# Second attention of a four-layer block: 64x64 products in quarters of the array, probabilities scaled instead of outputs, and a new order on every engine

## The reference

```python
qh = (q @ Wq).reshape(b, l, HEADS, HEAD_DIM).transpose(0, 2, 1, 3)
kh = (kv @ Wk).reshape(b, s, HEADS, HEAD_DIM).transpose(0, 2, 1, 3)
vh = (kv @ Wv).reshape(b, s, HEADS, HEAD_DIM).transpose(0, 2, 1, 3)
qh = rms_norm(qh, q_norm_w)
kh = rms_norm(kh, k_norm_w)
scores = jnp.einsum('bhld,bhsd->bhls', qh, kh) * (1.0 / np.sqrt(HEAD_DIM))
scores = jnp.where(mask, scores, NEG_INF)
attn = jax.nn.softmax(scores, axis=-1)
o = jnp.einsum('bhls,bhsd->bhld', attn, vh)
o = o.transpose(0, 2, 1, 3).reshape(b, l, HEADS * HEAD_DIM)
return o @ Wo
```

## Time and profile before

| | |
|---|---|
| median of 3 runs | 2405.72 us (2403.03 to 2406.18) |
| the profiled execution | 2402.11 us, span 2400.1 us |
| TensorE busy | 2088.1 us, 87% of the span |
| VectorE / ScalarE / GpSimd busy | 69% / 37% / 26% |
| the second attention | about 845 to 1380 us of the span |

### The profile page before, as it was taken

How to read it: one execution, slowest core, us unless ns; L and a number is a source line. 1 busy time by engine, 2 the same in 40 slices (tenths; PEclk the granted TensorE clock), 3 DMA queues, 4 the chain that set the end, 5 groups by cost and what they waited for, 6 DMA issues and landing times. The chain is left out here.

```text
span 2400.1 us, 39365 instructions
## 1 busy us (share of the span) xinstructions
PE 2088.1 (87%) x12809; PEld 1146.2 (48%) x12811; DVE 1658.4 (69%) x3378; ACT 881.2 (37%) x1559; POOL 613.7 (26%) x832
## 2 busy tenths in 40 slices
PE   4759999999999879999999899689979999768965
PEld 2634444444444446666666544245544444324531
DVE  4857776786787767777777589567746666436668
ACT  4522212201211056666666554223332222223335
POOL 4641110111111054545555332222200000111201
PEclk8569999999999989999999999789979999979985
DMA  3403203221320421111111000000003433210001
GB/s 103 149 1 72 55 19 70 54 62 26 71 54 17 107 85 35 33 34 32 35 31 36 23 1 1 1 12 12 11 19 94 109 80 84 56 27 13 12 3 36
DMA packets 131760, 106.43 MB, mean 44 GB/s; under 512 B 95400, under 2 KB 113704, under 8 KB 127152
## 3 DMA queue, kind: packets, MB, share of 16 engines
q1 hardware_dynamic: 131632, 104.84, 17.8%
HBM read 80.85 MB, written 2.97 MB: 35 GB/s over the span
## 5 line engine op out<-in xcount | busy, mean ns | idle before, releaser
L1020 PE MATMUL l0f_acc<-l0f_z,w_all 128*128 128x512 f32 x512 | 232.0, 615 | 22.7 <-DVE l0f_z L1232 22.7
L917 POOL TENSOR_TENSOR l0f_v<-l0f_val,l0f_top 64x256 f32<-64x256 f32 x128 | 78.4, 613 | 505.3 <-DVE l0f_val L1195 497.8
L971 PE MATMUL l0f_work<-w_all,l0f_xs 128*128 128x512 f32 x384 | 183.5, 600 | 9.9 <-DVE l0f_val L1190 8.6
L1020 PEld LDWEIGHTS l0f_acc<-l0f_z,w_all 128*128 128x128 f32 x512 | 100.2, 197 | 153.8 <-issue 126.0
L241 POOL TENSOR_SCALAR var_eps<-mean_var 128x4 f32<-128x4 f32 (+1 forms) x64 | 14.6, 229 | 540.6 <-DVE mean_var L225 538.8
L2268 PE MATMUL a_score<-keys_by_head,a_qT 128*64 128x512 f32 x512 | 143.0, 640 | 9.0 <-DMA keys_by_head<-w_all 9.0
L1195 DVE COPY_PREDICATED l0f_val<-l0f_oh,l0f_work 128x512 f32<-128x512 int32 x160 | 116.7, 729 | 23.7 <-PE l0f_work L971 7.5
L2760 DVE TENSOR_TENSOR l2f_hu<-l2f_act_g,l2f_pu 128x512 f32<-128x512 f32 x104 | 71.2, 685 | 68.8 <-ACT l2f_act_g L2686 67.5
L2686 ACT ACTIVATE l2f_act_g<-l2f_pg 128x512 f32<-128x512 f32 x104 | 61.5, 594 | 149.6 <-PE l2f_pu L2627 137.7
L2635 PE MATMUL l2f_acc<-l2f_hid,w_all 128*128 128x512 f32 x208 | 107.4, 598 | 10.4 <-DVE l2f_hid L2766 10.4
L1690 DVE TENSOR_REDUCE l1x_ms_k<-l1x_sq_k 128x8 f32<-128x512 f32 x64 | 43.9, 687 | 103.2 <-ACT l1x_sq_k L1576 103.2
(11 more groups left out here) (360 smaller groups left out, 4811.3 us busy)
## 6 DMA issues: line engine op xcount, KB each, us to landing
l0f_first_mask<-onehots SPq DMA_DIRECT2D x32, 512.0 KB, 5.7
w_all<-onehots SPq DMA_DIRECT2D x32, 512.0 KB, 11.8
l1x_v<-l1x_vr SPq DMA_DIRECT2D x256, 64.0 KB, 2.1
w_all<-combination SPq DMA_DIRECT2D x40, 256.0 KB, 5.2
w_all<-in_weights SPq DMA_DIRECT2D x1, 4640.0 KB, 17.4
l0x_m_b<-running_max SPq DMA_DIRECT2D x16, 256.0 KB, 4.6
keys_by_head<-w_all SPq DMA_DIRECT2D x256, 8.0 KB
keys_by_head<-ctxT_all SPq DMA_DIRECT2D x256, 8.0 KB
```

The costliest lines, as they stand in the source:

```text
L917: nc.gpsimd.tensor_tensor(v2[a * SEQ:(a + 1) * SEQ, t % 2, b, :, :], val[r, t % 2, :, :].rearrange("p (c a) k -> p c a k", a=2)[:, :, a, : ...
L971: nc.tensor.matmul(value_banks[e % 3][:, :], xs[:, t * P:(t + 1) * P], ve[:, e, :], start=True, stop=True).then_inc(ve_done, 1)
L1020: nc.tensor.matmul(acc[:, :], oe[:, n % E, n // E, :], z[:, n % Z, :], start=(n == 0), stop=(n == C * E - 1)).then_inc(acc_done, 1)
```

## The change

Scores: kT is a plain copy, and each head's 64x64 block is a product of its own, 64 input rows and 64 output partitions, 16 in all; the two heads of a chunk go to two banks of `score`. The mask is two instructions, one a bank. Values: the output comes out turned, straight from 16 products of 64x64x64 of `v2` and the turned probabilities, so `turn_out` and `og` go; therefore the probabilities are scaled (`scale_probs`) and not the outputs. The outputs share a PSUM bank with the projected v (`v_and_out`), so `project_v` of n waits for `copy_oT` of n-4, and `values` of n-3 for `copy_v` of n. The probabilities are turned into k's bank `turn1` and no longer into q's. `prob` has two buffers, `vr` and `v2` four. The zeroed tiles and their memsets go. The order on TensorE, ScalarE and VectorE is new; GpSimd's is the same.

```diff
--- before.py
+++ after.py
@@ -1288,23 +1288,22 @@
...
-        qT, kb = sb("qT", [P, C, P]), sb("kb", [P, C, 2, 2, SEQ])
-        vr = sb("vr", [P, 2, W])
-        v2 = sb("v2", [P, 2, 2, C, 2, HD])
+        qT, kT = sb("qT", [P, C, P]), sb("kT", [P, C, P])
+        vr = sb("vr", [P, 4, W])
+        v2 = sb("v2", [P, 4, 2, C, HD])
-        diff, prob = sb("diff", [P, HU, SEQ]), sb("prob", [P, HU, SEQ])
+        diff, prob = sb("diff", [P, HU, SEQ]), sb("prob", [P, 2, HU, SEQ])
-        og = sb("og", [P, HU, HD])
-        proj_q, proj_k, proj_v = ps("proj_q"), ps("proj_k"), ps("proj_v")
-        turn0, turn1, score, po, y = ps("turn0"), ps("turn1"), ps("score"), ps("po"), ps("y")
+        proj_q, proj_k, v_and_out = ps("proj_q"), ps("proj_k"), ps("v_and_out")
+        turn0, turn1, y = ps("turn0"), ps("turn1"), ps("y")
...
@@ -1334,17 +1333,16 @@
...
-                sp.wait_ge(v2_zero, count(2))
-                    after(sp, pv_done, n - 1)
+                    after(sp, pv_done, n - 3)
-                            sp.dma_start(v2[a * SEQ:(a + 1) * SEQ, j % 2, b, :, a, :],
-                                         vr[b * SEQ:(b + 1) * SEQ, j % 2, :].rearrange("p (c a e) -> p c a e", c=C, a=2)
-                                         [:, :, a, :]).then_inc(v_loaded[j % 2], 16)
+                            sp.dma_start(v2[a * SEQ:(a + 1) * SEQ, j % 4, b, :, :],
+                                         vr[b * SEQ:(b + 1) * SEQ, j % 4, :].rearrange("p (c a e) -> p c a e", c=C, a=2)
+                                         [:, :, a, :]).then_inc(v_loaded[j % 4], 16)
...
@@ -1416,7 +1412,8 @@
...
                     after(pe, vr_ready, n)
-                    nc.tensor.matmul(proj_v[:, :], cs[:, j // 4, tok], wv[:, h * W:(h + 1) * W], start=True, stop=True)\
+                    after(pe, oT_ready, n - 3)
+                    nc.tensor.matmul(v_and_out[:, :], cs[:, j // 4, tok], wv[:, h * W:(h + 1) * W], start=True, stop=True)\
...
-                    after(pe, pT_ready, n - 1)
-                    after(pe, oT_ready, n - 2)
+                    pe.wait_ge(pT_ready, count(max(n - 1, 0) if isinstance(n, int) else n - 1))
...
@@ -1450,49 +1446,44 @@
-                    nc.tensor.matmul(score[:, :], core.ident_bf[:, :],
-                                     bcast(mask[:, bass.ds(4 * g + j // 2, 1), :].rearrange("p one k -> p (one k)"), 1, HU),
-                                     start=True, stop=False, skip_group_check=True)
+                    key_mask = mask[:, bass.ds(4 * g + j // 2, 1), :].rearrange("p one k -> p (one k)")
+                    for a in range(2):
+                        nc.tensor.matmul(score[:, a, :], core.ident_bf[:, :], bcast(key_mask, 1, C),
+                                         start=True, stop=False, skip_group_check=True)
                     for c in range(C):
                         for b in range(2):
-                            q = slice(b * SEQ, (b + 1) * SEQ)
-                            ins = nc.tensor.matmul(score[q, c * P:(c + 1) * P], qT[:, c, q],
-                                                   kb[:, c, b, :, :].rearrange("p a k -> p (a k)"),
-                                                   start=False, stop=True, skip_group_check=True)
+                            for a in range(2):
+                                r, q = slice(a * HD, (a + 1) * HD), slice(b * SEQ, (b + 1) * SEQ)
+                                ins = nc.tensor.matmul(score[q, a, c * SEQ:(c + 1) * SEQ], qT[r, c, q], kT[r, c, q],
+                                                       start=False, stop=True, skip_group_check=True)
                     ins.then_inc(score_done, 1)
 
-                def turn_probs(n):
-                    pe.wait_ge(exp_done, count(n + 1))
-                    pe.wait_ge(qT_ready, count(at_most(n + 2, U * GROUPS)))
+                def turn_probs(g, j):
+                    n = U * g + j
+                    pe.wait_ge(prob_ready, count(n + 1))
+                    pe.wait_ge(kT_ready, count(at_most(n + 2, U * GROUPS)))
                     after(pe, pT_ready, n)
                     for c in range(C):
-                        ins = nc.tensor.transpose(turn0[:, c * P:(c + 1) * P],
-                                                  prob[:, 2 * c:2 * c + 2, :].rearrange("p a k -> p (a k)"),
+                        ins = nc.tensor.transpose(turn1[:, c * P:(c + 1) * P],
+                                                  prob[:, j % 2, 2 * c:2 * c + 2, :].rearrange("p a k -> p (a k)"),
                                                   core.const("ident"))
                     ins.then_inc(p_turned, 1)
 
                 def values(g, j):
                     n = U * g + j
                     pe.wait_ge(pT_ready, count(n + 1))
-                    pe.wait_ge(v_loaded[j % 2], 64 * (4 * g + j // 2 + 1))
-                    after(pe, og_ready, n)
+                    pe.wait_ge(v_loaded[j % 4], 64 * (2 * g + j // 4 + 1))
+                    pe.wait_ge(vr_ready, count(at_most(n + 4, U * GROUPS)))
+                    after(pe, oT_ready, n)
+                    pe.sem_inc(may_multiply, 1)
                     for c in range(C):
                         for b in range(2):
-                            q = slice(b * SEQ, (b + 1) * SEQ)
-                            ins = nc.tensor.matmul(po[q, c * P:(c + 1) * P], probT[:, c, q],
-                                                   v2[:, j % 2, b, c, :, :].rearrange("p a e -> p (a e)"),
-                                                   start=True, stop=True)
+                            for a in range(2):
+                                r = slice(a * SEQ, (a + 1) * SEQ)
+                                q = slice(b * SEQ, (b + 1) * SEQ)
+                                ins = nc.tensor.matmul(v_and_out[r, c * P + b * SEQ:c * P + (b + 1) * SEQ], v2[r, j % 4, b, c, :],
...
-                def turn_out(n):
...
                 def slot(g, j):
                     if live(g):
                         project_q(g, j)
+                    h, i = lagging(g, j, 3)
+                    if live(h):
+                        turn_probs(h, i)
+                    if live(g):
+                        project_v(g, j)
                     h, i = lagging(g, j, 1)
                     if live(h):
                         turn_q(U * h + i)
+                        turn_k(U * h + i)
+                    h, i = lagging(g, j, 3)
+                    if live(h):
+                        values(h, i)
                     if j % 4 in (3, 0):
                         h, i = lagging(g, j, 7)
                         if live(h):
                             project_out(h, i)
-                    if live(g):
-                        project_v(g, j)
-                    h, i = lagging(g, j, 1)
-                    if live(h):
-                        turn_k(U * h + i)
                     if j % 4 == 1:
...
-                    h, i = lagging(g, j, 2)
-                    if live(h):
-                        turn_probs(U * h + i)
-                    h, i = lagging(g, j, 3)
-                    if live(h):
-                        turn_out(U * h + i)
                     h, i = lagging(g, j, 1)
                     if live(h):
                         scores(h, i)
-                    h, i = lagging(g, j, 2)
-                    if live(h):
-                        values(h, i)
 
                 for g in range(2):
                     for j in range(U):
...
@@ -1584,69 +1570,62 @@
                 def copy_kT(n):
                     act.wait_ge(k_turned, count(n + 1))
                     after(act, score_done, n)
-                    for a in range(2):
-                        r = slice(a * HD, (a + 1) * HD)
-                        ins = nc.scalar.activation(kb[r, :, :, a, :],
-                                                   turn1[r, :].rearrange("p (c b k) -> p c b k", c=C, b=2), ACT.Copy,
-                                                   scale=core.col("l1_kw")[r, :])
-                    ins.then_inc(kT_ready, 1)
+                    nc.scalar.activation(kT[:, :, :], turn1[:, :].rearrange("p (c k) -> p c k", c=C), ACT.Copy,
+                                         scale=core.col("l1_kw")).then_inc(kT_ready, 1)
 
...
                 def copy_v(g, j):
                     n = U * g + j
                     act.wait_ge(v_done, count(n + 1))
-                    if not isinstance(g, int) or n > 1:
-                        act.wait_ge(v_loaded[j % 2], 64 * (4 * g + j // 2))
-                    nc.scalar.activation(vr[:, j % 2, :], proj_v[:, :], ACT.Copy).then_inc(vr_ready, 1)
-
-                def exp(n):
+                    if not isinstance(g, int) or n > 3:
+                        act.wait_ge(v_loaded[j % 4], 64 * (2 * g + j // 4))
+                    nc.scalar.activation(vr[:, j % 4, :], v_and_out[:, :], ACT.Copy).then_inc(vr_ready, 1)
+
+                def exp(g, j):
+                    n = U * g + j
```

(60 more changed lines are left out.)

33 lines of the change are left out of this document (13 added, 20 removed).

## The result

The changed kernel takes 2455.64 us (median of 4, 2452.2 to 2457.96) beside 2404.38 us for the kernel before (median of 4 on the same chip): ratio 1.0212, 95% interval 1.0194 to 1.023, so 1.9 to 2.3% slower. The profiled execution's span is 2455.2 us, 55.1 above that of before.

A forecast was written before the change was run, and what follows sets the result against it. VectorE's new order was taken to put both root trips in series: mean slot 8.54 us against 7.88, +42 us, plus 4.5 for half clock, giving 2448.6, or 2452 us as a median. The range was 2425 to 2490 us.

The forecast's parts named there:

- The slot: Second attention, eight heads of a 128-token tile: mean slot 8.54 us against 7.88, +42 us over 64 slots.
- The loop without projection: VectorE's order with q's and k's root trips through GpSimd in series, in slots without output projection: 8.47 us.
- The slots with a projection: Path from normalise k through turned keys, values, output projection and k's square to k's root: 8.61 us a slot.
- Values: TensorE's 16 products of 64x64x64 for the values: 1.08 us from start to next, +.10.
- Scores: TensorE's scores in four quadrants instead of two column halves: between .46 and 1.08 us, no effect on the time.
- TensorE's own queue: TensorE's work without waits: 6.9 to 7.5 us a slot; at 7.2, a 43 us gain if it still bounded.
- the faster rival: TensorE stays the bound from `project_q` to `scores` and the kernel is faster: -43 us, 2363 us; chance .09.
- busy share: TensorE waits before the turned keys for normalise k and is busy some 83% of the stage.
- The clock: TensorE's idling in the slots brings half clock; three costs of 1.5 us taken as an estimate, 4.5 us.
- a clock that falls often: Rival: idling brings half clock into most projection slots or other TensorE work, 2480 to 2530 us; chance .12.
- halves that take turns: Rival: the two halves of the values run in turn on TensorE, + 29 us, 2481; chance .02.
- The step that did not hold: VectorE's order: TensorE staying the bound is decided by whether sum k avoids waiting behind normalise q; -43 us if so.

The follow-up runs named there:

- run 2: Changed kernel with the output projection ahead of the turned q and keys on TensorE: 2444.96 us, ratio 1.0159 to the kernel before.
- run 4: Changed kernel with only totals and scaling ahead of normalise q on VectorE, sum of k still behind it: 2427.46 us, ratio 1.0094 to the kernel before.
- run 5: Changed kernel with one GpSimd instruction a root, leaving out the division by 64 and the 1e-5: 2422.14 us, ratio 1.0059 to the kernel before.
- run 12: Changed kernel with totals and scaling before normalise q, output projection before turned q, k's projection before values, its square before output copy, exponential before q/key copies: 2365.28 us.
- Run 1: Changed kernel with totals, scaling and sum of k ahead of normalise q on VectorE: 2439.44 us, ratio 1.0141 to the kernel before.
- run 7: Changed kernel with totals, scaling, sum of k before normalise q; output projection before turned q; k's projection before values, its square before output copy: 2445.69 us.
- run 8: Changed kernel: totals, scaling, k's sum before normalise q; output projection before turned q; k's projection before values, square before output copy; exponential before q/key copies: 2371.6 us.
- run 11: Changed kernel with totals, scaling, sum of k before normalise q; output projection before turned q and k; exponential before q and key copies: 2435.14 us, ratio 1.012.
- run 3: Changed kernel with totals, scaling and sum of k ahead of normalise q, and output projection ahead of turned q and keys: 2445.06 us, ratio 1.0163.
- run 9: Changed kernel with only the exponential moved ahead of the copies of turned q and keys on ScalarE: 2453.38 us, ratio 1.0197.
- run 10: Changed kernel with totals, scaling and sum of k ahead of normalise q, and the exponential ahead of the q and key copies: 2439.49 us, ratio 1.0138.

## Why the prediction was right, point by point

*The slot.* Predicted 8.54 us, measured 8.54 by the squares and 8.59 in the steady slots. The loop without projection was summed to 8.47 and is 8.42 (trips of 2.82 and 2.83 for 2.84, reciprocal .23 for .24). The slots with a projection were summed to 8.61 and are 8.76, for the way from `normalise_k` to the sum of k is 5.93 for 5.77: turned keys to values .59 for .44, values to k 2.91 for 2.81, k to its square 1.06 for 1.17, and .74 for .72 to the turned keys. The errors, -.05 and +.15, leave the steady mean .05 above the sum, 3 us over 64 slots; that the spacing of all squares agrees to the last digit is luck, for it counts the short first slots, which the sum did not treat apart. Runs 2, 4 and 5 show that the parts are what they were taken for: without the projection on k's way the slot is 8.41, with the totals under q's trip the slots are 7.67 and 8.76, and .28 less in each trip takes .59 from the slots in which both trips are on the path and .29 from those in which k's alone is.

*TensorE.* Values 1.08 (1112.05 to 1113.13), as predicted. Scores .62 (1114.58 to 1115.20), inside the bounds .46 to 1.08. TensorE's own queue was put at 7.2 us a slot; run 12, in which it is bound by it, has 7.30, and the time that the faster rival was given, 2363 us, is near that run's 2365.28. So the change does spare TensorE about what was reckoned; the new order hid it. Its busy share was put at some 83% of the stage and is 463.63 of 538 us, 86%.

*The clock.* A term that was off: 4.5 us for half clock in the steady slots, and the row of 873 to 1411 shows 1.00, so 0. Idling in pieces of up to 1.7 us, once a slot, did not lower it here. In its place, not foreseen, stands the drain, 6.9 us, of which 6.40 - 3.69 = 2.7 are the last two output projections at the lower clock; the start and the later stages hold 6.2 more, within the spread of the traces. Of the span's 55.1 us the slots' 42.0 were forecast; the 4.5 stood in for a part of the other 13.1 for the wrong reason, so the last 4 us of the agreement are luck. In all 2452 was predicted and 2455.64 measured. The rivals with a clock that falls often and with halves that take turns fall by the same rows: granted clock 1.00, values 1.08.

*The step that did not hold* is not in the sum but in the faster rival: "It decides when sum k does not wait behind normalise q". Run 1 took that wait away and stayed at 2439.44; run 12 kept it and reached 2365.28. What decides is how much lies in the loops as a whole: the totals between the two roots (runs 4 and 12), and the exponential and k's square between one use of q's bank and the next (runs 7, 8 and 11). The prediction looked for loops through `normalise_k` only. The others, through the bank of q, were not on the path in the changed kernel; they came with the cure.

*What stays open.* The expectation for run 12 named the waits of q that it would remove and a cost of about as much; with the intervals of runs 8 and 12 overlapping, whether that edit gains anything isn't settled. Why the drain is longer by 6.9 us, and in which orders its clock falls, was not tried; the last two output projections took 3.69 us in some of the other kernels and 5.4 to 6.6 in the rest. That loop A and B are what holds runs 3 and 11 is shown by runs 7 to 12 together; that the first run sits on B in its slots with a projection rests on its equality with run 10 and on 9.17 us from one projection of q to the next in a slot with projection (1106.93 to 1116.10 in its trace), B's length.

## What to carry to other kernels

Where an engine's order is written by hand, sum each closed loop that goes through a blocking wait, and also those that go through a single buffer's release; a moved step can cut one loop and make another of the same length. An edit that gives nothing alone says only that something as long stands beside it: the edits that cut the two parallel loops here gave 0 and 10 us alone and 74 together. If a change removes work from the bound engine and the kernel gets slower, look at the order before giving the change up: here 51 us slower became 41 us faster by moving steps only.

## What was not expected of the hardware

The scores' 32 instructions take .62 us from start to next, the values' 32 of the same shape 1.08. The scores use all four pairs of input half and output half, 4 products in each; the values use two, since head `a` reads the input rows of half `a` and writes the partitions of half `a`, 8 in each. A projection of 512 columns takes .86 us, so 64 columns would take .11 by themselves (an estimate from that row): 4 in a quarter .43, 8 in a quarter .86, and all 16 one after the other 1.72. The scores lie .19 and the values .22 above their fullest quarter, and both well below 1.72. That fits a time that goes by the fullest quarter and not by the count; it is not isolated, for the scores write two banks and the values one.

The Trainium skill, TensorEngine Tiling (Array Packing), section Restrictions and Gotchas, says that different row tiles cannot access one bank at the same time. The two halves of the values read different input rows and write one bank, and their 16 products take 1.08 us where one after the other would be 1.72. The measurement decides: in this form they do not take turns. No run here put them in two banks.

TensorE kept its full clock, the 2.4 GHz level, through 873 to 1411 us, busy 463.63 of 538 us and waiting up to 1.7 us at a time in the steady 400 us, while in the drain of the same stage, with 17.23 us busy of 25, the mean of its two levels was .71.
